# Masked cross attention in a fused kernel: score products in three rounded parts, key parts made by GpSimd, two weights loaded later

## The reference, cut to what matters

```python
x = x + _L0_xattn_ref(_layernorm(x), ctx_1024, ...)      # cross attention, rotary
x = x + _L0_attn_ref(_layernorm(x), ...)                 # causal self attention, 16 heads of 32
x = x + _L0_ffn_ref(_layernorm(x), weight)               # x @ sign(weight)
# the fourth block, _L1_xattn_ref(q=layernorm(x), encoder_k=encoder_v=ctx_1024, mask, wo_w, wo_b):
scores = jnp.einsum('bhqd,bhkd->bhqk', qh, kh) + encoder_attention_mask
weights = jax.nn.softmax(scores, axis=-1)
ctx = jnp.einsum('bhqk,bhkd->bhqd', weights, vh)
ctx = ctx.transpose(0, 2, 1, 3).reshape(q.shape[0], q.shape[1], -1)
return jax.nn.relu(ctx @ wo_w.T + wo_b)
# then a causal self attention with 16 heads of 64 and eight experts of width 2048
```

## Time and profile before

| | us |
|---|---|
| median of 3 runs | 1193.22 |
| lowest, highest | 1191.4, 1197.19 |
| the profiled execution | 1196.15 |
| its span, first to last instruction | 1194.4 |
| mean granted TensorE clock in it, share of full | 0.994 |
| TensorE busy | 1174.4 (98%) |
| VectorE, ScalarE, GpSimd busy | 688.8, 540.1, 217.0 |

### The profile page before, as it was taken

The page is one execution under the profiler, slowest core; times in us unless marked ns, Lnnn a source line. Parts: engine busy times, 40 slices in busy tenths (PEclk is TensorE's granted clock), DMA queues, the critical chain, the costliest instruction groups (busy, mean ns, idle before and its releaser), DMA issues.

```text
span 1194.4 us, 23415 instructions
## 1 busy us (share of the span) xinstructions
PE 1174.4 (98%) x9888; PEld 963.8 (81%) x9888; DVE 688.8 (58%) x1220; ACT 540.1 (45%) x907; POOL 217.0 (18%) x178
## 2 busy tenths in 40 slices
PE   8999999999999999999899999999999999999998
PEld 6888888888788888864546667888899999999997
DVE  4654554545464533466788885265765566566562
ACT  4433324332433322224359997373644544444441
POOL 2243343444333443350000000010000000000000
PEclk9999999999999999999989999999999999999999
DMA  8210201010100020245232324301545445445440
GB/s 302 71 55 1 66 2 52 4 36 19 36 19 2 27 72 1 83 139 212 96 152 79 136 108 178 142 1 72 228 159 211 161 192 211 157 195 207 158 162 19
DMA packets 28160, 126.06 MB, mean 106 GB/s; under 512 B 2715, under 2 KB 2971, under 8 KB 17572
## 3 DMA queue, kind: packets, MB, share of 16 engines
q1 hardware_dynamic: 28068, 124.74, 27.9%
HBM read 124.20 MB, written 0.52 MB: 104 GB/s over the span
## 4 chain that ended last, share of the span: by engine, by line
PE 49%; issue 2%; DVE 2%; ACT 2%; DVEq 0%
PE mid_bk L57 11%; PE mid_bk L58 10%; PE mid_bk L59 10%; PE mid_bk L1105 5%; PE mid_bk L1120 2%; PE mid_bk L1150 2%; PE mid_bk L1076 2%; PE mid_bk L995 2%; PE mid_bk L1140 1%; PE mid_bk L1249 0%; ACT sa_sc L1415 0%; PE mid_bk L1201 0%; PE mid_bk L1190 0%; PE mid_bk L1050 0%; PE mid_bk L986 0%
## 5 line engine op out<-in xcount | busy, mean ns | idle before, releaser
L565 POOL TENSOR_TENSOR norm_both<-norm_both,prob 128x512 f32<-128x512 f32 x118 | 155.4, 1317 | 145.6 <-DVE prob L357 138.2
L494 ACT ACTIVATE prob<-u_ps 128x512 f32<-128x512 f32 x128 | 66.2, 605 | 181.5 <-PE u_ps L667 181.5
L57 PE MATMUL mid_bk<-mo_x_hi,mo_w_hi 128*128 128x256 f32 x496 | 141.0, 284 | 0.0
L58 PE MATMUL mid_bk<-mo_x_lo,mo_w_hi 128*128 128x256 f32 x496 | 141.0, 284 | 0.0
L59 PE MATMUL mid_bk<-mo_x_hi,mo_w_lo 128*128 128x256 f32 x496 | 141.0, 284 | 0.0
L340 DVE TENSOR_TENSOR turned<-k_ps,tabs 128x512 f32<-128x512 f32 x32 | 22.1, 690 | 189.7 <-PE k_ps L59 189.6
L1788 DVE TENSOR_TENSOR mo_w_lo<-w_raw,mo_w_hi 128x2048 fp32r<-128x2048 f32 x32 | 73.3, 2292 | 72.7 <-ACT mo_w_hi L1497 72.7
L57 PE MATMUL k_ps<-ctx_hi,wk_hi 128*128 128x512 f32 x256 | 102.8, 402 | 0.0
L57 PE MATMUL u_ps<-wv_hi,ctx_hi 128*128 128x512 f32 x256 | 101.7, 397 | 0.8 <-ACT prob L494 0.8
L483 ACT ACTIVATE vals<-u_ps 128x512 f32<-128x512 f32 x64 | 38.3, 598 | 141.2 <-PE u_ps L59 141.1
L1497 ACT ACTIVATE mo_w_hi<-w_raw 128x2048 fp32r<-128x2048 f32 x32 | 61.2, 1913 | 87.9 <-PE mid_bk L59 87.9
(11 more groups left out here) (264 smaller groups left out, 2357.2 us busy)
## 6 DMA issues: line engine op xcount, KB each, us to landing
w_raw<-in_w SPq DMA_DIRECT2D x64, 1024.0 KB, 6.3
ctx_raw<-in_ctx_rows SPq DMA_DIRECT2D x8, 1024.0 KB, 5.5
x_k<-in_ctx_T SPq DMA_DIRECT2D x8, 1024.0 KB, 7.0
x_val<-in_ctx_heads SPq DMA_DIRECT2D x8, 1024.0 KB, 5.0
tabs<-in_rot_tabs SPq DMA_DIRECT2D x8, 512.0 KB, 3.8
vals<-in_wq_rows SPq DMA_DIRECT2D x4, 512.0 KB, 7.6
ctx_raw<-in_wo SPq DMA_DIRECT2D x1, 2048.0 KB, 9.7
x_mask<-in_mask SPq DMA_DIRECT2D x2, 1024.0 KB, 9.0
```

The source lines that it names most:

```text
L57: pe.matmul(out, w_hi, x_hi, start=start, stop=False)
L58: pe.matmul(out, w_hi, x_lo, start=False, stop=False)
L494: act.activation(prob[:, t % 2, i, :], u_ps[:, i, :], ACT.Exp).then_inc(s["exped"], 1)
L565: ins = pool.tensor_tensor(to, to, src, ALU.add)
```

## The change

1. **Scores in three rounded products.** `scores(t)` multiplies parts in a rounded 32-bit format (F32R, shown as fp32r). Query and key are split into a high part (rounded) and a low part (the rest): q_hi x k_hi, q_hi x k_lo and q_lo x k_hi are added in the same bank. One rounded product is one matmul instruction. A step has 12, in three rounds of four heads.
2. **Key parts on GpSimd.** Ahead of each step GpSimd makes k_hi (a copy that rounds) and k_lo (raw minus high, written over the raw key), each 128 x 512. A piece needs its group's key to have landed; TensorE waits for the piece (`k_split`). Two high buffers lie over space that is free then, one over `wo`.
3. **Query parts.** ScalarE writes q_hi from PSUM; for batch 1 it also still writes `normed_T`. q_lo of batch 0 is made by VectorE from PSUM (`low_query`, between add_values(1) and moments(4, 1)), that of batch 1 by GpSimd from `normed_T` ahead of piece 8. The query of batch 0 is turned into another bank, and the sign product that reuses this bank waits for q_lo.
4. **Two weights later.** `wo1` (1 MB) and `sa1_wk` (2 MB) are issued behind the last scores, since the new parts lie in their space.
5. The semaphore `bo_in` of the first block is merged into `consts_in`, with the same transfer and the same wait.

```diff
         x_gate = place("x1_gate", [1, NST, 4], 62.5)
+        k_hi = [place(f"x1_k_hi{r}", [P, S], (54.5, 128)[r], F32R) for r in range(2)]
+        k_lo = place("x1_k_lo", [P, 2, S], 141, F32R)
+        q_hi, q_lo = ([place(f"x1_q_{n}{b}", [P, KD, P], kb + 2 * b, F32R) for b in range(NB)]
+                      for n, kb in (("hi", 16), ("lo", 20)))
...
+            pool.wait_ge(s["rope"], 24)
+            pool.wait_ge(s["score"], NB)
+            pool.wait_ge(s["proj"], 6)
+            for t in range(NST):
+                n, c = t // 4, t % 4
+                if c == 0:
+                    pool.wait_ge(s_k[n % 2], 16 * (n // 2 + 1))
+                if t == 8:
+                    pool.wait_ge(s["T_out"], 6)
+                    pool.tensor_tensor(q_lo[1][:], normed_T[:, :, P:2 * P], q_hi[1][:], ALU.subtract).then_inc(x["q_lo"], 1)
+                cols = slice(c * 512, (c + 1) * 512)
+                pool.tensor_copy(k_hi[n % 2][:, cols], k_raw[:, n % 2, cols]).then_inc(x["k_split"], 1)
+                pool.wait_ge(x["k_split"], 2 * t + 1)
+                pool.tensor_tensor(k_lo[:, n % 2, cols], k_raw[:, n % 2, cols], k_hi[n % 2][:, cols],
+                                   ALU.subtract).then_inc(x["k_split"], 1)
...
             def scores(t):
                 n, c = t // 4, t % 4
                 b, g = n // 4, n % 4
-                if c == 0:
-                    pe.wait_ge(s_k[n % 2], 16 * (n // 2 + 1))
+                cols = slice(c * 512, (c + 1) * 512)
+                pe.wait_ge(x["k_split"], 2 * t + 2)
                 if t >= LAG:
                     pe.wait_ge(x["masked"], 4 * t)
-                for a in range(4):
-                    if 1 <= t < LAG:
-                        pe.wait_ge(x["masked"], 4 * (t - 1) + a + 1)
-                    rows = slice(32 * a, 32 * a + 32)
-                    pe.matmul(s_ps[:, a, :], normed_T[rows, g, b * P:(b + 1) * P],
-                              k_raw[rows, n % 2, c * 512:(c + 1) * 512], start=True,
-                              stop=True).then_inc(x["score"], 1)
+                for m in range(3):
+                    if t % 16 == 0 and m == 2:
+                        pe.wait_ge(x["q_lo"], b + 1)
+                    for a in range(4):
+                        if 1 <= t < LAG and m == 0:
+                            pe.wait_ge(x["masked"], 4 * (t - 1) + a + 1)
+                        rows = slice(32 * a, 32 * a + 32)
+                        part_k = (k_hi[n % 2][rows, cols], k_lo[rows, n % 2, cols], k_hi[n % 2][rows, cols])[m]
+                        ins = pe.matmul(s_ps[:, a, :], (q_hi, q_hi, q_lo)[m][b][rows, g, :], part_k, start=(m == 0),
+                                        stop=(m == 2))
+                        if m == 2:
+                            ins.then_inc(x["score"], 1)
...
-            turn_norm(3, 0, 0, 3)
+            turn_norm(3, 0, 1, 1)
...
+            def keep_query(j, b, side, bank):
+                act.wait_ge(s["T"], j + 1)
+                turned_norm = bk[side][:, bank, :].rearrange("p (k t) -> p k t", k=KD)
+                if b == 1:
+                    act.activation(normed_T[:, :, P:2 * P], turned_norm, ACT.Copy)
+                act.activation(q_hi[b][:], turned_norm, ACT.Copy).then_inc(s["T_out"], 1)
...
+            def low_query(j, side, bank):
+                dve.wait_ge(s["T_out"], j + 1)
+                dve.tensor_tensor(q_lo[0][:], bk[side][:, bank, :].rearrange("p (k t) -> p k t", k=KD), q_hi[0][:],
+                                  ALU.subtract).then_inc(x["q_lo"], 1)
```

More of the change, by code:

```diff
@@ L175, in cross_attention_rotary @@
                  "wv_hi", "wv_lo", "wk_hi", "wk_lo", "v_mm", "v_out", "k_mm", "rope", "score", "exped", "clipped",
-                 "summed", "weighed", "o_out", "den_mm", "den_out", "recip", "normalised", "y", "added", "bo_in", "bo_added", "rounded", "idle_set")
+                 "summed", "weighed", "o_out", "den_mm", "den_out", "recip", "normalised", "y", "added", "bo_added", "rounded", "idle_set")
         s = {n: sem("x0_" + n) for n in names}
@@ L406, in _ @@
                 if t == 28:
-                    dve.wait_ge(s["bo_in"], 16)
+                    dve.wait_ge(consts_in, 64)
                     for b in range(NB):
@@ L782, in latents @@
     x = {n: sem("x1_" + n) for n in
-         ("score", "gate", "masked", "top", "exped", "pT", "act_out", "dve_out", "pv", "den", "spread",
+         ("score", "gate", "k_split", "q_lo", "masked", "top", "exped", "pT", "act_out", "dve_out", "pv", "den", "spread",
           "wide", "wide_out", "normed", "y")}
@@ L834, in latents @@
         x_rden = place("x1_rden", [P, 2, 4], 54)
-        x_gate = place("x1_gate", [1, NST, 4], 62)
+        x_gate = place("x1_gate", [1, NST, 4], 62.5)
+        k_hi = [place(f"x1_k_hi{r}", [P, S], (54.5, 128)[r], F32R) for r in range(2)]
+        k_lo = place("x1_k_lo", [P, 2, S], 141, F32R)
+        q_hi, q_lo = ([place(f"x1_q_{n}{b}", [P, KD, P], kb + 2 * b, F32R) for b in range(NB)]
+                      for n, kb in (("hi", 16), ("lo", 20)))
         x_sc = place("x1_sc", [P, 2, 4, S], 64)
@@ L919, in _ @@
                 load_values(n)
-            sp.wait_ge(s["rope"], 24)
-            sp.dma_start(wo[:], rows("wo1")).then_inc(w_in, 16)
             sp.dma_start(wo_row[:], I["wo1_row"]).then_inc(w_in, 16)
@@ L924, in _ @@
             sp.wait_ge(s["y"], NB)
-            for n in ("sa1_wq", "sa1_wk"):
-                sp.dma_start(env[n][:], rows(n)).then_inc(env["sa1_w_in"], 16)
+            sp.dma_start(env["sa1_wq"][:], rows("sa1_wq")).then_inc(env["sa1_w_in"], 16)
             load_keys(2)
@@ L932, in _ @@
             sp.wait_ge(x["score"], 4 * NST)
+            sp.dma_start(wo[:], rows("wo1")).then_inc(w_in, 16)
+            sp.dma_start(env["sa1_wk"][:], rows("sa1_wk")).then_inc(env["sa1_w_in"], 16)
             sp.dma_start(env["sa1_wv"][:], rows("sa1_wv")).then_inc(env["sa1_w_in"], 16)
@@ L1055, in signs @@
                 pe.wait_ge(s["signed"], 1)
+                if j == 4:
+                    pe.wait_ge(x["q_lo"], 1)
                 for part_of in (sg_hi, sg_lo):
@@ L1536, in _ @@
             root(3, 0)
-            keep_norm(3, 0, 0, 3)
+            keep_query(3, 0, 1, 1)
             root(4, 1)
@@ L1914, in _ @@
             add_values(1)
+            low_query(3, 1, 1)
             moments(4, 1)
```

4 lines of the change are left out of this document (2 added, 2 removed).

## The result

| | before | changed |
|---|---|---|
| median (12 runs each, same chip), us | 1193.18 | 1196.77 |
| lowest, highest, us | 1191.4, 1197.31 | 1195.43, 1198.23 |
| the profiled execution and its span, us | 1196.15, 1194.4 | 1196.61, 1194.8 |
| mean granted clock in it | 0.994 | 0.991 |

The medians lie 3.6 us apart. The ratio, which weighs all twelve runs of each, is 1.0025 with the 95% interval [1.0014, 1.0036], and makes 3.0 us (1.7 to 4.3). That is within the 0.5% named as "no change that shows", but it is told from no change at all, and it has the other sign than the -0.75 us forecast.

A forecast was written before the change was run, and what follows sets the result against it. TensorE was taken as the bound, 98% busy, in a closed loop with VectorE's masks. Terms -4.75 + 2.4 + 1.0 - 0.2 + 0.8 = -0.75 us gave 1192.5 us from 1193.22; range 1186.5 to 1200.5, about 0.8.

The forecast's parts named there:

- no change that shows: Whole kernel: forecast of 1192.5 us, a difference under 0.5% (6 us) from the median of 1193.22; within 0.5%: 0.62.
- steps 1 to 6: Early steps: 0.8 us lost to loop order, 1.0 gained around step 2; sum -0.2 us, bounds -1 and +2.
- the steady steps: Steps 7 to 31: overlapping rounded products cut the score from 1.07 to 0.88 us, 25 steps, -4.75 us.
- the denominators: Group 0, after step 8's masks: two small SBUF-only VectorE instructions wait for GpSimd, +0.8 us, bounds 0 and 1.9.
- no overlap: Rival, scores: rounded products in different row groups run one after another, 2.7 us a step, 1249 us; chance 0.07.
- no shorter rounds: Rival, scores: three rounds no shorter than the f32 products, only start costs left, +4.0, 1197.2 us; chance 0.13.
- disturbed masks: Rival, from step 8 on: masks wait for GpSimd, about 1.1 us a piece, +26, 1219 us; chance 0.06.
- GpSimd ahead of the first mask: Start: five VectorE instructions wait for GpSimd's pieces 0 to 7, +2.4 us, bounds 0 and 4.9.
- the random hit: Start: a VectorE instruction meeting GpSimd's 2.1 us cycle at a random moment waits 0.49 us on average; five make 2.4.
- low_query: Ahead of the first mask: VectorE waits for ScalarE's query, then works 0.61 us; cost 1.0 us, not under 0.6.
- if the low clock lasts: Into step 6: three products at half speed cost 0.7 us more each; tied to the +2 bound.
- Transfers, ScalarE and the rest: Later weights, key pieces, ScalarE's second query write and merged semaphore: nothing lost; wo lands 2 us before the projection.

The follow-up runs named there:

- b1_pool: Kernel before with GpSimd's 32 pieces added, results unused, products still f32: 1194.07 us, ratio 1.0007.
- e1_gated: Changed kernel with GpSimd's piece 0 held until after centred(2, 0) and piece 3 until after centred(4, 1): 1194.16 us, ratio 1.0008.
- e2_lowq: Changed kernel with low_query behind moments(4, 1) instead of ahead of it: 1195.14 us, ratio 1.002.
- typical: Second profile of the kernel before, unchanged: profiled execution 1191.62 us, span 1189.9, clock 0.999; median of its timed runs 1193.11 us, ratio 1.0003.
- e4_all: Changed kernel with GpSimd's first pieces held back, low_query behind moments(4, 1) and heads as outer loop in steps 1 to 6: 1191.62 us, ratio 0.9985.
- e5_again: Second set of runs, on another chip, of e5_warm's kernel: 1189.13 us, ratio 0.997.
- e3_heads: Changed kernel with heads as the outer loop and the three parts as the inner loop in steps 1 to 6: 1195.47 us, ratio 1.0021.
- b2_cold: Kernel before without the eight filling products of idle(n) in steps 0 to 6: 1195.58 us, ratio 1.0022.
- a1_warm: Changed kernel with one filling product between scores(0) and the next turn, nothing else: 1196.77 us, ratio 1.0035.
- e5_warm: e4_all's kernel with one more filling product between scores(0) and the next turn: 1189.08 us, ratio 0.9966.

## Why the prediction was wrong, and where it was right

Two steps of the sum failed, mainly on TensorE's clock: the term for steps 1 to 6, forecast at -0.2 and measured at +2.8 us, and a term for the clock ahead of the first mask, which the sum didn't have and which measured 1.8 us. And the sum was counted from a profile that itself held such stretches. The other terms came out near their sizes, or, in the steady steps, erred against each other.

**The steady steps: the mechanism right, the exact sum by luck.** Score 0.88 forecast, 0.90 measured; -4.75 + 0.8 for the denominators makes -3.95, and the stretch from step 7 to the last mask got 3.96 us shorter. Both terms were too large: 24 steps lie between these two masks, at 0.17 us each they give 4.1, and the denominators cost some 0.1 (one of eight small additions took 419 ns for 158). The two errors cancel. The rivals of no overlap and of no shorter rounds fell by that row (they would decide from 1.15 and 1.03 us on), the one of disturbed masks by the 693 ns.

**GpSimd ahead of the first mask: right in size.** 2.4 us forecast from the random hit, 2.2 measured. That is luck in part: b1_pool shows 0.8 for nearly the same pieces, so this agreement holds for one phase and the bounds of 0 to 4.9 were the honest part. GpSimd's pieces are also quicker than I had them (1.9 us, not 2.1).

**low_query: right.** 1.0 forecast; 1.4 in the changed kernel, 1.0 in e1_gated, and e2_lowq takes 1.0 of it back. It was priced as one step of VectorE's path, and the experiment shows that its place in the order decides it.

**The clock ahead of the first mask: a step that was missing.** 1.8 us. I priced GpSimd's stretching as a delay of VectorE alone. It also left TensorE idle longer in two places. TensorE's timeline, the changed kernel and then the typical one, with the idle time ahead in brackets:

```profile
582.45 0.67 PE L1047 MATMUL mid_bk<-ident,sa_sc 128*128 128x128 f32 x4 [2.88 <-DVE sa_sc L1680]
584.55 1.11 PE L1004 MATMUL mid_bk<-ident,norm_both 128*128 128x128 f32 x4 [1.43 <-DVE norm_both L1643]
```
```profile
580.57 0.66 PE L1029 MATMUL mid_bk<-ident,sa_sc 128*128 128x128 f32 x4 [1.62 <-DVE sa_sc L1648]
581.82 0.66 PE L986 MATMUL mid_bk<-ident,norm_both 128*128 128x128 f32 x4 [0.59 <-DVE norm_both L1611]
```

The granted clock is 1.00 in 578 to 583 and 0.51 in 583 to 590 of the changed kernel; already the turn at 584.55 takes 1.11 us for 0.66. That GpSimd's stretching brings this on is likely but not shown. All four profiles of kernels in which it stretches scaled(1, 3) to 1.72 or 1.73 us have 0.66 to 0.83 in 580 to 590; but so have three without any such stretching (the first of before, e4_all, e5_again: 0.83, with idle times of 1.62 or 1.63 and 0.60 us on TensorE), and six others without it have 1.00. The 1.8 us are measured; their cause stays open.

**Steps 1 to 6: the term that was wrong.** I forecast -0.2, with +2 as the bound "if the low clock lasts"; measured against the typical profile it is +2.76. The parts that come of the loop order were near the forecast: 0.84 - 0.39 = 0.45 us more ahead of step 5 (0.4 forecast), and step 6 alike; with step 1, which was not priced, e3_heads takes 1.3 us out of the stretch where I had 0.8. The 1.0 us that three rounds were to gain around step 2 had nothing to be gained from: the 3.09 us of idle time there is 0.32 in the typical profile. Instead the clock is at 0.50 in 600 to 610, and the stretch is 2.76 us longer than typical. Taken away one after the other, in the profiles, the order of the loops gives 1.3 us (26.03 to 24.76) and the whole clock 2.2 (24.75 to 22.5), which leaves the rounded products 0.8 under typical. The bound of +2 named the cause and was a little small; what failed is that I took the low clock for a fixed stretch of the program, to stay where the profile had it.

**Counting from a profile and taking it from the median: the largest error.** I took the first profile's 2.93 us above the median for a constant. Against that profile the sum was nearly right: from its +4.38, -0.03 and -3.95 us in the three stretches (+0.40) I had +3.4, -0.2 and -3.95 (-0.75). But the 2.93 us were low-clock stretches in the very place of the change. The changed kernel's profile has such stretches too, all its twelve executions show a mean clock of 0.989 to 0.992 (before mostly 0.998 or 0.999), and none is under 1195.4. Its profile lies 0.16 us under its median. So 3.1 of the 4.3 us by which the forecast missed are this offset, and 1.2 are terms of the sum. A hint was there: with three runs at 1191.4, 1193.2 and 1197.2 and a profile at 1196.15, a granted clock of 0.50 in a stretch that the change touches should have raised the question whether it belongs to the kernel.

**Transfers, ScalarE and the rest: right.** The projection starts without a wait; key pieces are in time; ScalarE idles 0.20 us ahead of its turned chunks in a step without denominators and isn't the bound.

The profiles side by side, each column as in the table of the result, with the granted clock in 580 to 590:

| us | start | steps 0 to 6 | steady | clock |
|---|---|---|---|---|
| first profile of before | 18.11 | 26.06 | 102.20 | 0.83 |
| typical before | 17.15 | 23.27 | 102.21 | 1.00 |
| b1_pool, GpSimd's pieces added | 17.96 | 23.27 | 102.21 | 1.00 |
| b2_cold, no filling products | 17.15 | 26.40 | 102.20 | 1.00 |
| changed | 22.49 | 26.03 | 98.25 | 0.66 |
| a1_warm, changed with one more filling product | 21.35 | 25.92 | 99.68 | 0.83 |
| e2_lowq | 20.95 | 26.50 | 98.26 | 0.66 |
| e3_heads | 21.57 | 24.76 | 98.42 | 0.69 |
| e1_gated | 18.15 | 26.80 | 98.23 | 1.00 |
| e4_all | 18.86 | 24.75 | 98.36 | 0.83 |
| e5_warm | 17.54 | 22.52 | 98.20 | 1.00 |
| e5_again, the same kernel | 18.86 | 22.50 | 98.39 | 0.83 |

What sets the low stretches to one place or another is only partly settled. Shown is that a filling product in e4_all (e5_warm) takes the one in steps 1 to 6 away and gives 2.5 us, that leaving filling products out of before costs 2.4, and that a single one moves a stretch by 10 us in the changed kernel. Not shown is what brings on the one at 583: the same program has it in one execution and not in another (first and typical profile of before, e5_warm and e5_again), with the same idle times on TensorE around 581.

## What to carry to other kernels

Look at the granted clock in the stretch that a change touches, and hold the profiled execution against the list of times, before a wait in it is booked as a gain. A helper engine that is off the path is paid where the path's small SBUF-only instructions are, so start its work behind them (a wait on a semaphore that counts them was worth 2.0 us here by the ratios, 2.6 by the medians). And where a change gives back less than its steady part should, look at the few steps ahead of the steady stretch: here 4 us were gained in the steady steps, and 8 us lost in the 20 us ahead of the first mask and the 26 us behind it. Three small edits of order and one filling product won most of them back.

## What was unexpected of the hardware

- Rounded products in four row groups overlap: twelve in 0.90 us, the second and third round 0.24 us apart, against eight f32 instructions in 1.07 us.
- One kernel, unchanged, has executions from 1191.4 to 1197.3 us in the first set, most near 1191.6, 1193.2 and 1196; the slower profile differs from the quick one by two stretches with a granted clock of 0.50 between 580 and 604 us.
- The cost of the same GpSimd pieces for the same five VectorE instructions was 2.8 us of stretching in one kernel and 1.4 in another (0.22 + 0 + 0.16 + 0.97 + 0.02). Which of the two engines is held up goes by which starts first: 0.03 us decided it beside scaled(1, 3). A copy of GpSimd that takes 0.61 us took 1.08 behind it.
- One filling product is worth 2.5 us in the repaired kernel and nothing that shows in the changed kernel and in the kernel before.
